# A decoder layer on one core: the per-row quantisation step rewritten as two-tensor instructions, and all five engine orders and PSUM banks chosen anew

## The reference, cut to what matters

```python
x = _layernorm(x + _L0_attn_ref(x, ...), axis=-1)       # 16 heads of 32, causal
x = _layernorm(x + _L0_xattn_ref(x, ctx_1024, ...), axis=-1)
x = _layernorm(x + _L0_ffn_ref(x, W_g, W_u, W_d), axis=-1)

def activation_quant(x):
    s = 127.0 / jnp.max(jnp.abs(x), axis=-1, keepdims=True)
    return jnp.clip(jnp.round(s * x), -128, 127) / s
xq = activation_quant(rms_norm(x))
g = jax.nn.silu(ternary_matmul(xq, W_g))      # ternary_matmul: x @ sign(w).T
u = ternary_matmul(xq, W_u)
return ternary_matmul(g * u, W_d)
```

## Time and profile before

| | |
|---|---|
| median of 3 runs | 581.6 us (581.37 to 583.06) |
| the profiled execution: its time | 582.68 us |
| its span | 580.9 us |
| busy: PE, DVE, ACT, POOL | 550.0, 478.7, 420.7, 381.3 us |
| mean granted clock of PE | 0.989 of full speed |

### The profile page before, as it was taken

One profiled execution on the slowest core, in us unless ns is written; L12 is line 12 of the kernel. 1 busy time (PEld: TensorE's weight loads), 2 busy tenths in 40 slices (PEclk: granted clock), 3 DMA queues, 4 the chain that ended last, 5 costly groups with the idle time before them and its releaser, 6 DMA issues.

```text
span 580.9 us, 14215 instructions
## 1 busy us (share of the span) xinstructions
PE 550.0 (95%) x5324; PEld 356.2 (61%) x5324; DVE 478.7 (82%) x1252; ACT 420.7 (72%) x789; POOL 381.3 (66%) x409
## 2 busy tenths in 40 slices
...
GB/s 303 304 332 186 272 244 261 81 55 91 137 65 183 138 120 181 191 173 93 90 110 160 136 160 100 199 144 87 43 117 164 143 188 178 137 109 37 24 33 36
DMA packets 220516, 84.29 MB, mean 145 GB/s; under 512 B 207008, under 2 KB 211616, under 8 KB 218912
## 3 DMA queue, kind: packets, MB, share of 16 engines
...
...
...
## 4 chain that ended last, share of the span: by engine, by line
PE 47%; DVE 14%; POOL 4%; ACT 2%; issue 2%; DMA 2%; POOLq 0%; DVEq 0%; ACTq 0%; SPq 0%
PE ps_b L665 17%; PE ps_b L813 15%; PE ps_b L828 11%; DVE ps_b L1086 3%; PE ps_b L757 2%; PE ps_b L721 2%; POOL ph L1275 2%; DVE xq L1179 2%; DVE scaled L1176 2%; DVE bn L1019 1%; DVE rows L1214 1%; DMA x1T<-rhl 1%; DMA oT<-ohl 1%; ACT p L910 1%; POOL rstd L1250 1%
## 5 line engine op out<-in xcount | busy, mean ns | idle before, releaser
L1275 POOL TENSOR_TENSOR ph<-p,ph 128x768 f16<-128x768 f32 (+1 forms) x84 | 152.5, 1821 | 80.5 <-ACT ph L846 43.4
L910 ACT ACTIVATE p<-ps_b,tops 128x128 f32<-128x128 f32 (+3 forms) x256 | 120.2, 550 | 25.4 <-issue 15.3
L1086 DVE CUSTOM_DVE_ANT_0 ps_b<-ps_b,future 128x128 f32<-128x128 f32 (+3 forms) x256 | 117.6, 521 | 9.4 <-PE ps_b L721 9.2
L813 PE MATMUL ps_b<-xqT,sg 128*128 128x256 f16 x1024 | 119.1, 273 | 0.9 <-DVE rows L1214 0.6
L828 PE MATMUL ps_b<-sd,hp 128*128 128x512 fp8e4 x512 | 117.1, 379 | 0.0
L813 PEld LDWEIGHTS ps_b<-xqT,sg 128*128 128x128 fp8e4 x1024 | 98.4, 98 | 19.3 <-issue 1.8
L1271 POOL TENSOR_TENSOR hp<-gt,hp 128x512 f16<-128x512 f32 x64 | 74.1, 1161 | 38.9 <-ACT hp L846 38.7
L665 PE MATMUL ps_b<-xhl,wh 128*128 128x256 f16 x480 | 84.2, 275 | 1.0 <-POOL xhl L1275 0.5
L828 PEld LDWEIGHTS ps_b<-sd,hp 128*128 128x128 f16 x512 | 48.6, 98 | 54.8 <-issue 2.4
L846 ACT ACTIVATE ph<-p 128x768 f16<-128x768 f32 (+1 forms) x72 | 66.2, 926 | 3.5 <-DMA pt<-ph 3.3
L665 PE MATMUL ps_b<-xhl,wl 128*128 128x256 f16 x240 | 65.9, 275 | 0.0
...
## 6 DMA issues: line engine op xcount, KB each, us to landing
...
pt<-ph SPq DMA_TRANSPOSE x84, 4.3
...
```

What stands on the lines that cost most here:

```text
L813: ins = pe.matmul(ps[:, a * HALF:(a + 1) * HALF], sg[:, ("gg", "uu").index(name), c, ht * P:(ht + 1) * P], xqT[:, c, :], start=c == 0, sto ...
L910: ins = act.activation(p32[:, n % P32_SLOTS, to:to + keys], ps[:, col:col + keys], ACT.Exp, scale=-1.0, bias=tops[:, s % 2, g, j, qt % 2:q ...
L1086: ins = dve.tensor_tensor_reduce(scores, scores, future[:, S - width:S], EXP_SCALE, 3e38, ALU.add, ALU.min, tops[:, s % 2, g, j, qt % 2:qt ...
L1275: pool.tensor_tensor(out_, in_, hi, ALU.subtract).then_inc(signal, 1)
```

## The change

Three things change. `quantise` computes `normed` directly behind the reciprocal, ahead of `scaled` and `xq`. Its two instructions of 128x512 elements become scalar_tensor_tensor: the constants 1.5 * 2^23 and 127 come as a second tensor, a column of the new buffer `levels` read with step 0 over 512 elements, in place of immediate numbers; two more memsets on POOL fill it. And all five order tables and all bank numbers are new: the tables hold the same tasks, of which 356 of PE's 494, 363 of DVE's 645, 401 of ACT's 662, 106 of POOL's 300 and 55 of SP's 210 stand at another place.

```diff
-CONSTS = 8
+CONSTS = 10
...
-tw0.0.2.0.0@0,2 mx0.0.3.0@4,7,3,1 pv0.0.1.2@5 pv0.0.1.3@5 qk0.1.3@6 tw0.0.3.0.0@7,0 pv0.0.2.0@3 pv0.0.2.1@3
...
+mx0.0.3.0@7,4,5,3 pv0.0.1.2@0 pv0.0.1.3@0 qk0.1.3@2 tw0.0.2.0.0@1,7 tw0.0.3.0.0@0,4 mx0.1.0.0@6,5,3,2 pv0.0.2.0@1
...
+        levels = sb("levels", [P, 2], F32)
...
                 wait(dve, a_step, s, t + 1)
                 dve.reciprocal(scale, step).then_inc(a_scale.sem, 1)
-                wait(dve, a_scale, s, t + 1)
-                wait_for(dve, wx_lo, 1)
-                dve.tensor_scalar(scaled[:, :], row, scale, MAGIC, ALU.mult, ALU.add).then_inc(a_magic.sem, 1)
-                wait(dve, a_magic, s, t + 1)
-                wait(dve, xqT_out[t], s, 0)
-                dve.tensor_scalar(xq[:, t, :], scaled[:, :], MAGIC, 127.0, ALU.subtract, ALU.min)\
-                   .then_inc(xq_out.sem, 1)
                 wait(dve, ln_rstd[2], s, t + 1)
                 wait(dve, invb_out, s - 1, 0)
                 dve.tensor_scalar(normed, step, root, DSCALE, ALU.mult, ALU.mult).then_inc(a_norm.sem, 1)
+                wait(dve, a_scale, s, t + 1)
+                wait_for(dve, wx_lo, 1)
+                wait_for(dve, consts, CONSTS)
+                magic, limit = (levels[:, i:i + 1].to_broadcast([P, D]) for i in range(2))
+                dve.scalar_tensor_tensor(scaled[:, :], row, scale, magic, ALU.mult, ALU.add).then_inc(a_magic.sem, 1)
+                wait(dve, a_magic, s, t + 1)
+                wait(dve, xqT_out[t], s, 0)
+                dve.scalar_tensor_tensor(xq[:, t, :], scaled[:, :], MAGIC, limit, ALU.subtract, ALU.min)\
+                   .then_inc(xq_out.sem, 1)
...
+                const(pool.memset(levels[:, 0:1], MAGIC))
+                const(pool.memset(levels[:, 1:2], 127.0))
```

More of the change, by code:

```diff
@@ L121 @@
[L121 to L140, removed]
@@ L146 @@
[L146 to L150, removed]
@@ new lines @@
+dn0.0.0.3@0 dn0.0.1.3@4 cp1.0@6 cp1.1@5 gg0.1.2@2 gg0.1.1@7 en1.0@0 en1.1@1 ib1@4 gg0.1.0@6 pv1.0.1.3@3 uu0.1.0@5
+qk1.1.3@4 en1.2@0 uu0.1.1@1 uu0.1.3@3 gg0.1.5@6 pv1.0.2.0@7 pv1.0.2.1@7 pv1.0.2.2@7 pv1.0.2.3@7 pv1.0.3.0@5
+pv1.0.3.1@5 pv1.0.3.2@5 uu0.1.2@4 pv1.0.3.3@5 gg0.1.4@1 gg0.1.3@0 dn0.1.0.0@7 en1.3@2 uu0.1.4@4 uu0.1.7@5 uu0.1.5@0
+uu0.1.6@3 dn0.1.0.1@7 gg0.1.7@2 gg0.1.6@1 dn0.1.1.0@4 dn0.1.1.1@4 dn0.1.0.2@7 mx1.1.0.1@6,0,1,3 op1.0.0@2
+mx1.1.1.0@5,6,0,1 op1.0.1@2 dn0.1.0.3@7 dn0.1.1.2@4 mx1.1.1.1@3,5,6,0 pv1.1.0.0@2 pv1.1.0.1@2 xm1.0.0@1
@@ new lines @@
+hi1.0.0.0.0 ex1.0.1.0 ex1.0.1.1 hi1.0.0.0.1 ex1.0.1.2 ex1.0.1.3 hi1.0.1.0.0 qk1.1.0 qk1.1.1 ex1.0.2.0 ex1.0.2.1
+hi1.0.1.0.1 ex1.0.2.2 ex1.0.2.3 hi1.0.2.0.0 hh0.0.6 ov1.0.0 hh0.0.7 hi1.0.2.0.1 ex1.0.3.0 ex1.0.3.1 ex1.0.3.2
+ex1.0.3.3 hi1.0.3.0.0 n10.1.0 hi1.0.3.0.1 va1.1.1 n10.1.1 cs1.0 cs1.1 qk1.1.2 ex1.1.0.0 ex1.1.0.1 ex1.1.0.2
+hi1.1.0.0.0 ex1.1.0.3 hi1.1.0.0.1 cp1.0 cp1.1 zn0.0.0 zn0.0.1 ib1 en1.0 en1.1 ov1.0.1 ga0.1.0 ga0.1.1 ez1.0 ez1.1
+ta1.0 qk1.1.3 hh0.1.0 ta1.1 en1.2 xs2.0.0 ez1.2 hh0.1.1 ov1.0.2 xs2.0.1 ga0.1.2 ta1.2 ov1.0.3 hh0.1.2 ga0.1.3 to1.0.0
```

327 lines of the change are left out of this document (171 added, 156 removed).

## The result

The changed kernel took 588.58 us (median of 5 runs, 587.23 to 588.87); the kernel before took 581.93 beside it (5 runs, 581.37 to 584.47). The ratio is 1.0099, with a 95% interval of 1.0076 to 1.0122: **slower by 1%**, where I forecast 577.0 and a range of 572 to 584. The profiled execution took 588.82, with a span of 587.0.

What follows compares the result with a forecast made beforehand. PE was taken as the bound, busy 550.0 of 580.9 us, so only its idle time and lower clock could change. Gains of 9.8 less costs of 5.1 gave 4.7 us less: 577 us, own range 574 to 580, final range 572 to 584.

Steps and rivals of the forecast that it cites:

- (a): First gate of step 6: `xq` comes later with longer tiles, so PE starts at 509.5, not 508.6; cost 0.9 us.
- (b): Step 7, built like step 6, with 1 us in hand: cost 0.3 us.
- (c): `cp1.0` takes bank 6 of `qk1.1.2`, which now queues behind the tile `n20.1.1`: cost 0.5 us.
- (d): `mx2.1.0.0` now waits for `qk2.1.0` behind the tile `n21.1.1`: cost 1.0 us, taken between 0 and 2.9.
- PE ends up behind the longer quantisation: Rival: in every step PE is delayed by the two longer tiles, giving 584.6 us; chance 0.13.
- (1): PE at 57 to 64: `lo0.0.3` goes ahead of four block maxima, scores restart earlier; 0.9 us gained, lower clock stays.
- (2): `ib0` waited for an exponential on bank 1; now bank 6, due earlier: 1.1 us gained.
- no change: the gaps close and open at other banks: Rival: PE runs into ACT and DVE again, so the 9.8 us gained is lost: 581.6 us; chance 0.20.
- (e): `qk3.0.3` takes bank 7 of `qk3.0.1`, queued behind the tile `n22.0.1`: cost 1.2 us, from 0 to 2.7.
- (f): `cp3.0` takes the bank of `qk3.1.1` behind tile `n22.1.1`, and `ib5` comes earlier: cost 1.2 us, 0 to 2.4.
- (5): At 303.7 `pv` waits for the first exponential, not the third: 1.4 us gained, plus 1.7 for the low clock at 305.
- Half rate: Rival: each rewritten instruction takes 1.2 us, 17 us in all, half on PE's path: 585.5 us; chance 0.07.

Runs made afterwards that it cites:

- old_orders_column_first: The kernel before, with its old orders and instructions, only `normed` moved ahead of `scaled` and `xq`: 579.1 us, ratio 0.9946 to the kernel before.
- new_orders_column_first: The changed kernel with the instructions of before in place of the two-tensor ones, `normed` still first: 580.8 us, ratio 0.9973 to the kernel before.
- splits_first: The old-orders, `normed`-first kernel with f16 rounding (0.9933), with the read-out `lo0.0.3` moved ahead of four block maxima on DVE: ratio 0.9937.
- banks_read_first: `new_orders_column_first` (0.9973) with DVE's read-outs `qk3.0.1` and `qk3.1.1` moved ahead of the quantised tiles `n22.0.1` and `n22.1.1`: ratio 0.9991.
- the two parts: `old_orders_column_first` with two-tensor instructions in step 3 alone, ratio 1.0003 (3.3 us), and in all steps but step 3, ratio 0.9993 (2.7 us).

## Why the prediction was wrong

Against the terms, by the ratios: I had the time at 4.7 us less, of which the two-tensor instructions were +1.7 (in a, b, c) and everything else -6.4. Measured are +7.3 and -1.6. So both halves failed, the first by 5.6 and the second by 4.8 us.

**The step that failed first: "what of the longer quantisation lies on PE's path".** I priced the rewrite right (7.4 us of DVE, 7.1 measured with the kept waits), and then put only 1.7 us of it on PE's path, in (a) to (c), taking DVE's 102 idle us as cover for the rest. Measured are 7.3. Step 3 shows how, with the old orders: its tile is followed by block maxima, exponentials and `pv` with no slack, and it cost 3.3 us. I had this tile in (d) alone, for the wait of `mx2.1.0.0`, taken at 1.0 of at most 2.9. In `old_orders_column_first` PE has no gap at that `pv` at all, and that was no proof of slack: the margin was about nothing. My rival "PE ends up behind the longer quantisation", priced 584.6 with 0.13, was the right mechanism, though still 4 us short, and in the new orders it is spread as that rival says: the n-th matmul of the changed kernel comes later than the same one of `new_orders_column_first` by 0.6 us at 112, 1.7 at 185, 3.6 at 276, 4.1 at 381, 6.6 at 449 and 8.5 at 517 (the two profiled executions; 1.7 of it is one more stretch at the lower clock).

**The second: "Sum 9.8".** Each of (1) to (6) was about right in place: the gaps (2) to (6) closed but for 0.38 at (2), and (1) was confirmed alone at 0.75. Wrong was to add them as if what PE gains at a place stayed with it. PE works behind DVE and ACT nearly everywhere; freed at one bank, it runs until the next thing that those two owe it. In the changed kernel new gaps stand near most of the closed ones (the one at 79 is 1.84 to 1.98 in all four kernels with the new orders, and 0.68 to 1.42 with the old), and `splits_first` and `banks_read_first` show it for single moves. The rival "no change: the gaps close and open at other banks" described the orders, at 1.0000 (0.9979 to 1.0020) when they are alone; I gave it 0.20.

**The costs by term.** (a) 1.5 to be seen before the gate of step 6, 2.22 measured, plus a low clock behind it (1.7) that I had not counted. (b) and (c): no gap at either place, though 1.63 stands behind `cp1.1`. (d) no gap, taken at 1.0. (e) 1.76, taken at 1.2. (f) 2.72 and a low clock behind it, taken at 1.2, range to 2.4: here the tile lay beside POOL, its two instructions taking 1.60 and 2.50 in the changed kernel:

```profile
437.02 1.60 DVE L1182 SCALAR_TENSOR_TENSOR scaled<-rows,amax,levels 128x512 f32<-128x512 f32 x1
438.65 2.50 DVE L1185 SCALAR_TENSOR_TENSOR xq<-scaled,levels 128x512 f16<-128x512 f32 x1
```

I had (a) down to the longer tiles, but `new_orders_column_first`, without the rewrite, has 1.85, 1.46 and 2.19 at (a), (e) and (f) already. So these waits come mostly from the orders, and the rewrite adds 0.37, 0.30 and 0.53 to them: the rest of its 7.3 us lies in the clock and at places that I did not name.

**The clock.** The low stretch at 305 is gone in all four kernels with the new orders, as (5) has it. Of the 7 us at about 63 the changed kernel has 3.5, but the three others with these orders have 6.8. In place of what went, 3.4 us came at 442 and again at 514. I had counted a drop only where it could go, never behind the gaps that I forecast myself.

**Half rate**, as my rival had it (1.2 us, half of one element a nanosecond), is refuted for two f32 SBUF sources too: 0.69 us is the minimum of the f32-and-column `xq`, the same as for f32 with f16 in the earlier trace rows. But I compared with the wrong rate. The rows, 0.69 us for 512 elements and 2.29 for 2048, give about 1.04 ns an element and a fixed 0.16 us; with the same fixed part (an estimate) the one-source `xq` of 0.43 us took 0.53 ns an element. The one-source instruction is the fast one, and the second tensor takes that away. The rule of the Trainium skill, "Vector Engine (DVE) Microarchitecture Reference", section "Points that are easy to get wrong", that this instruction with two such sources halves its throughput, does not say half of what: read against the one-source instruction the trace agrees with it, and my statement that the rows disagree was a misreading.

**What stays open.** How the 7.9 us divide into DVE's plain extra time, its longer stretches beside POOL and the clock is settled only in part, for step 3: 3.3 and 2.7 for the two parts leave 1.9 of 7.9, within the uncertainty of the three ratios. Which of the other places take the 7.3 us with the new orders was not tested by an experiment. A rewrite whose second tensor does not lie in SBUF was not tried, since all eight PSUM banks are in use.
